# Half of the score masks by ScalarE and GpSimd, a first sequence without attention, start-up matmuls, and two PSUM banks each for attention and experts

## The reference

```
x = L0_attn_x                                   # (8, 256, 128)
# A: retention, 8 heads, key 16 wide, value 32 wide
qr, kr = rotate(q), rotate(k)                   # q*cos + swap_pairs(q)*sin
qk  = einsum('bhik,bhjk->bhij', qr, kr) * mask  # mask: causal decay
qk  = qk / clip(abs(qk.sum(-1)), 1.0)
out = einsum('bhij,bhjd->bihd', qk, v)
out = out * rsqrt(mean(out*out) + eps)
x   = x + (silu(g) * out) @ wo
# B: S = the 8 sequences, 16 heads, 4 key-value heads, head 8 wide
scores = where(causal, einsum(q, k) / sqrt(HD), min)
h1  = h + softmax(scores) @ v @ proj_weight.T
# C: router
logits = layer_norm(h1) @ router_weight ; top_p, top_i = top_k(softmax(logits), 2)
# M: experts, capacity 640 tokens
fc1 = gelu(xt @ moe_w1[e]) ; fc2 = fc1 @ moe_w2[e]
out = x + h1 + sum over the two experts of gate * fc2
```

## Time and profile before

| of the profiled execution | |
|---|---|
| its time | 242.57 us, of which the span of the trace is 240.8 us |
| TensorE clock granted, mean | 0.986 of full |
| PE busy | 216.7 us (90%) |
| PE weight loads busy | 183.6 us (76%) |
| DVE busy | 180.1 us (75%) |
| ACT busy | 146.1 us (61%), of which 46.2 us are 36 table loads |
| POOL busy | 94.8 us (39%) |
| first matmul starts at | 6.25 us |
| first expert matmul starts at | 48.0 us |

### The profile page before, as it was taken

One profiled execution on the slowest core, in us unless ns is written; L12 is line 12 of the kernel. 1 busy time (PEld: TensorE's weight loads), 2 busy tenths in 40 slices (PEclk: granted clock), 3 DMA queues, 4 the chain that ended last, 5 costly groups with the idle time before them and its releaser, 6 DMA issues.

```text
span 240.8 us, 4945 instructions
## 1 busy us (share of the span) xinstructions
PE 216.7 (90%) x1744; PEld 183.6 (76%) x1744; DVE 180.1 (75%) x543; ACT 146.1 (61%) x268; POOL 94.8 (39%) x121
## 2 busy tenths in 40 slices
PE   0677868899999999989999999999999989989995
PEld 0456545688887878877888889998798869879994
DVE  1466788695989789899996998697749864895533
ACT  2162763778868756946973876586746465827431
POOL 0021345334558642528623850582465136521000
PEclk9977999999999999999999999999999999999999
DMA  6992000000000000000000000000000000000000
GB/s 178 292 319 57 4 0 0 4 0 3 0 3 3 0 25 0 3 1 3 1 0 25 0 0 4 22 3 0 22 3 1 23 0 4 22 3 0 23 3 22
DMA packets 8073, 6.46 MB, mean 27 GB/s; under 512 B 752, under 2 KB 7152, under 8 KB 8048
## 3 DMA queue, kind: packets, MB, share of 16 engines
q1 hardware_dynamic: 8048, 6.14, 8.8%
HBM read 5.09 MB, written 1.05 MB: 25 GB/s over the span
## 4 chain that ended last, share of the span: by engine, by line
PE 54%; DVE 16%; issue 14%; POOL 9%; ACT 4%; DMA 1%; DVEq 0%; POOLq 0%; ACTq 0%
PE bank L773 16%; PE bank L784 13%; POOL prod L293 5%; PE bank L672 3%; DVE ao L930 3%; PE bank L621 3%; PE bank L699 3%; PE bank L638 2%; DVE res L1036 2%; PE bank L684 2%; ACT L445 2%; POOL qk L369 2%; PE bank L629 1%; PE bank L691 1%; DVE sm L866 1%
## 5 line engine op out<-in xcount | busy, mean ns | idle before, releaser
L773 PE MATMUL bank<-x2T,w 128*128 128x256 f32 x256 | 64.4, 386 | 1.6 <-DVE res L1036 1.6
L784 PE MATMUL bank<-w,hT 128*128 128x128 f32 x512 | 64.7, 277 | 0.0
L784 PEld LDWEIGHTS bank<-w,hT 128*128 128x128 f32 x512 | 61.7, 192 | 3.0 <-issue 1.1
L583 ACT ACTIVATE hT<-bank 128x512 f32<-128x512 f32 x64 | 37.5, 598 | 23.6 <-PE bank L773 23.5
L773 PEld LDWEIGHTS bank<-x2T,w 128*128 128x128 f32 x256 | 45.3, 190 | 8.1 <-DVE res L1036 3.1
L1036 DVE SCALAR_TENSOR_TENSOR res<-bank,gate,res 128x128 f32<-128x128 f32 x128 | 38.4, 341 | 16.7 <-PE bank L784 15.4
L445 ACT ACT_TABLE_LOAD x36 | 46.2, 1283 | 4.4 <-DVE mv L812 3.7
L293 POOL TENSOR_TENSOR prod<-qkv 128x128 f32<-128x128 f32 (+7 forms) x16 | 22.3, 1413 | 36.6 <-ACT qkv L455 36.6
L866 DVE TENSOR_TENSOR sm<-bank,con 128x512 f32<-128x512 f32 x32 | 19.9, 683 | 5.1 <-PE bank L672 5.0
L301 POOL TENSOR_TENSOR prodv<-attn_exp,qkv 128x128 f32<-128x128 f32 (+7 forms) x16 | 18.7, 1188 | 9.2 <-ACT attn_exp L551 9.2
L376 POOL TENSOR_TENSOR qkc<-qk,kcum 128x256 f32<-128x256 f32 x8 | 5.8, 730 | 31.0 <-DVE kcum L852 31.0
(11 more groups left out here) (109 smaller groups left out, 378.8 us busy)
## 6 DMA issues: line engine op xcount, KB each, us to landing
x<-in_x SPq DMA_DIRECT2D x8, 128.0 KB, 4.3
w<-in_w SPq DMA_DIRECT2D x1, 1024.0 KB, 5.8
...
```

The source lines that it names most:

```text
L583: eng.activation(hT[:, n % NM], m_banks[n % NM][:].rearrange("p (t n) -> p t n", t=NF), ACT.Gelu_apprx_tanh).then_inc(sem("gelu"), 1)
L773: last = mm(m_banks[n % NM][:, t * SLEN:(t + 1) * SLEN], w1[:, e, t * P:(t + 1) * P], x2T[:, i], start=True, stop=True)
L784: last = mm(m_banks[n % NM][:, c * D:(c + 1) * D], hT[:, n % NM, t, c * P:(c + 1) * P], w2[:, e, t], start=(t == 0), stop=(t == NF - 1))
```

## The change

- Masks: from the third sequence on (i >= 2) the four masks are split. Banks 2 and 3 are masked by DVE as before. Banks 0 and 1 are copied to SBUF by ACT (`a_lift`), and POOL multiplies the copies by the triangle in place (`a_cut`). The next sequence's `a_T` and `a_qk` wait for the copies. For the first two sequences DVE masks all four, in the order 2, 3, 0, 1.
- `a_out` is split: the state part and heads 4 to 7 run once the first two masks are there, heads 0 to 3 in `a_out_rest`.
- The first sequence's B has no scores, softmax or products: ACT copies its value row into the place of the attention result.
- `NB` is 2 and `NM` is 2.
- `a_rowsums` issues its two matmuls with 64 rows each, in separate halves of the array's rows and into separate banks (f0 and f1, now one tensor `front`).
- Six matmuls on a tile of zeros (`p_warm`): four ahead of the first `a_T`, two more before `a_kT:0` and `a_scores:0`. In `a_rstd` the table load stands ahead of the wait.
- `a_qkc`, `a_weight`, `b_core` of sequences 0 and 1 and the products of sequence 1 move from POOL to DVE.
- In B the scores are stored with the sequence index innermost, so `b_max` and `b_sum` read neighbours.
- `ORDER` is a new table.

```diff
-NB = 1
-NM = 3
+NB = 2
+NM = 2
+MASK_ORDER = (2, 3, 0, 1)
...
+p_warm:0 p_warm:1 p_warm:2 a_stats:0 p_warm:3 a_aggr:0 a_rstd:0 a_xh:0 a_T:0 a_xT:0 a_qk:0 a_vmm:0 a_rotate:0
+a_v:0 a_g:0 a_rotated:0 p_warm:4 a_tanh:0 a_kcum:0 a_kT:0 a_knat:0 a_qo:0 a_qkc:0 a_state_mm:0 a_silu:0
...
+            def a_cut(i):
+                if i < VECTOR_FIRST:
+                    return
+                for r in range(2):
+                    eng.wait_ge(sem("lifted"), lifts(i) + r + 1)
+                    heads_of = sm[:, r].rearrange("p c h n -> p (c h) n")
+                    eng.tensor_tensor(heads_of, heads_of, tri.unsqueeze(1).to_broadcast([P, 4, P]),
+                                      ALU.mult).then_inc(sem("cut"), 1)
...
+                exp_ln()
                 eng.wait_ge(sem("a_aggr"), NC * (group[-1] + 1))
                 if i == 0:
                     eng.wait_ge(sem("eps"), 2)
-                exp_ln()
...
+            def a_lift(i):
+                if i < VECTOR_FIRST:
+                    return
+                for r in range(2):
+                    eng.wait_ge(sem("scores"), 4 * i + r + 1)
+                    copy(sm[:, r].rearrange("p c h n -> p (c h n)"), score_banks[r][:], "lifted")
...
                 eng.wait_ge(sem("qkv"), i + 1)
+                if i == 0:
+                    for c in range(NC):
+                        own = b_banks[i][:, c * QKV + D + KVD:(c + 1) * QKV]
+                        copy(aon[:, c].rearrange("p (r f) -> p r f", r=QPK),
+                             own.unsqueeze(1).to_broadcast([P, QPK, KVD]), "own_value")
...
+            def p_warm(i):
+                if i == 0:
+                    eng.wait_ge(sem("warm"), 1)
+                mm(m_banks[0][:, 0:SLEN], warm[:, 0:P], warm[:], start=True, stop=True)
...
-                if i >= 1:
-                    eng.wait_ge(sem("sm"), 4 * (i - 1) + 1)
+                if 1 <= i <= VECTOR_FIRST:
+                    eng.wait_ge(sem("sm"), masks(i - 1) + 3)
+                if i > VECTOR_FIRST:
+                    eng.wait_ge(sem("lifted"), lifts(i - 1) + 1)
...
                 for u in range(2):
-                    last = mm(f1[:, u * SLEN:(u + 1) * SLEN], same_head[:, u * P:(u + 1) * P], qkc[:],
+                    rows = slice(u * D // 2, (u + 1) * D // 2)
+                    last = mm(front[:, u, 0:SLEN], same_head[rows, u * P:(u + 1) * P], qkc[rows, :],
                               start=True, stop=True)
...
             def a_out(i):
-                eng.wait_ge(sem("sm"), 4 * (i + 1))
+                eng.wait_ge(sem("sm"), masks(i) + 2)
+                eng.wait_ge(sem("state"), i + 1)
...
+                heads(i, range(4, RH))
+            def a_out_rest(i):
+                if i < VECTOR_FIRST:
+                    eng.wait_ge(sem("sm"), masks(i + 1))
+                else:
+                    eng.wait_ge(sem("cut"), lifts(i + 1))
+                heads(i, range(4)).then_inc(sem("o"), 1)
...
             def a_mask(i):
-                for r in range(4):
+                for r in MASK_ORDER if i < VECTOR_FIRST else (2, 3):
```

More of the change, by code:

```diff
@@ L53 @@
-a_weight:1 c_stats:0 c_aggr:0 c_rstd:0 a_g:2 a_qo:2 c_core:0 a_s2:2 a_og:1 c_T:0 c_x2T:0 a_wo:1 c_logits:0
-a_x1:1 m_fc1_0:0 a_aggr:6 c_best:0 a_tanh:2 c_where:0 c_ahead:0 b_stats:1 m_fc1_1:0 m_gelu_0:0 c_onehot:0
-b_aggr:1 c_half:0 a_aggr:7 m_fc2_0:0 b_sub:1 c_select:0 m_gelu_1:0 a_silu:2 c_base:0 c_rank:0 c_gsel:0
-a_scores:2 c_gate:0 m_acc_0:0 b_rstd:1 m_fc1_2:0 a_mask:2 b_core:1 a_T:3 b_T:1 a_xT:3 m_fc2_1:0 b_l1T:1 b_qkv:1
-m_acc_1:0 a_out:2 m_gelu_2:0 b_kv:1 m_fc2_2:0 b_prod:1 a_osq:2 b_scores:1 a_ms:2 b_hid:1 b_max:1 a_qk:3 a_tt:2
@@ L78 @@
-a_state_mm:6 b_aoT:3 a_kcum:6 a_qo:6 b_proj:3 a_state:6 a_wo:5 a_qkc:6 b_h1:3 c_base:2 c_stats:3 a_rowsums:6
-a_x1:5 b_rstd:4 c_base:3 c_aggr:3 m_fc2_6:1 a_silu:6 c_rstd:3 b_core:4 a_s2:6 m_acc_5:1 c_cum:2 a_scores:6
-c_core:3 m_acc_6:1 c_T:3 a_mask:6 m_fc1_0:2 m_gelu_7:1 c_x2T:3 a_T:7 m_gelu_0:2 c_logits:3 m_fc2_7:1 a_xT:7
-c_best:3 a_vmm:7 c_where:3 c_ahead:3 c_onehot:3 c_half:3 c_select:3 c_rank:3 c_gsel:3 m_fc1_1:2 b_stats:5
-c_gate:3 m_acc_7:1 b_T:4 m_fc2_0:2 b_aggr:5 b_l1T:4 a_v:7 b_qkv:4 m_acc_0:2 a_qk:7 b_kv:4 m_gelu_1:2 b_prod:4
@@ new lines @@
+a_mask:0 a_out:0 a_out_rest:0 a_T:1 a_xT:1 a_osq:0 a_qk:1 a_vmm:1 a_rotate:1 a_ms:0 a_v:1 a_tt:0 a_rotated:1
+a_ln:0 a_kT:1 a_kcum:1 a_rs:0 a_knat:1 a_weight:0 a_qo:1 a_state_mm:1 a_g:1 a_og:0 a_stats:4 a_qkc:1 a_wo:0
+a_tanh:1 a_silu:1 a_aggr:3 a_state:1 a_x1:0 a_rstd:2 a_rowsums:1 b_stats:0 a_s2:1 b_aggr:0 a_stats:5 b_sub:0
+b_rstd:0 a_stats:6 a_scores:1 a_aggr:4 b_core:0 b_hid:0 a_mask:1 b_T:0 a_xh:2 b_l1T:0 b_qkv:0 a_T:2 a_out:1
+a_xT:2 a_aggr:5 b_kv:0 a_out_rest:1 a_qk:2 a_osq:1 a_ms:1 a_rotate:2 b_aoT_mm:0 a_vmm:2 b_aoT:0 b_proj:0 a_tt:1
@@ new lines @@
+a_v:2 a_rotated:2 b_h1:0 a_g:2 a_ln:1 a_aggr:6 a_rs:1 a_kcum:2 a_kT:2 a_knat:2 a_weight:1 a_state_mm:2 c_stats:0
+a_qkc:2 a_og:1 a_xh:3 a_tanh:2 a_state:2 a_wo:1 a_qo:2 a_silu:2 c_base:0 a_rowsums:2 a_x1:1 a_stats:7 a_s2:2
+a_aggr:7 b_stats:1 a_scores:2 b_aggr:1 c_aggr:0 b_sub:1 a_lift:2 a_mask:2 a_cut:2 a_T:3 a_xT:3 a_qk:3 a_out:2
+a_xh:4 c_rstd:0 b_rstd:1 c_core:0 a_out_rest:2 a_rstd:4 b_core:1 a_vmm:3 a_osq:2 a_rotate:3 b_hid:1 c_T:0 a_ms:2
+a_v:3 c_x2T:0 b_T:1 a_rotated:3 c_logits:0 a_tt:2 b_l1T:1 m_fc1_0:0 c_best:0 a_ln:2 a_kcum:3 a_kT:3 a_rs:2
@@ new lines @@
+a_scores:4 m_gelu_7:0 a_lift:4 m_fc1_0:1 a_mask:4 a_cut:4 c_logits:1 b_max:2 m_fc2_7:0 a_T:5 b_exp:2 m_acc_7:0
+a_out:4 b_prodv:2 a_xT:5 c_best:1 b_rstd:3 c_where:1 a_out_rest:4 c_onehot:1 a_qk:5 c_select:1 c_ahead:1 c_cum:1
+b_ao:2 c_half:1 m_gelu_0:1 b_sub:3 a_vmm:5 c_base:1 c_rank:1 b_sum:2 a_v:5 m_fc1_1:1 b_core:3 c_gsel:1 b_hid:3
+m_fc2_0:1 m_gelu_1:1 c_gate:1 a_osq:4 a_g:5 m_acc_0:1 b_norm:2 a_ms:4 a_tanh:5 a_rotate:5 b_aoT_mm:2 m_fc1_2:1
+m_fc2_1:1 m_gelu_2:1 a_rotated:5 b_T:3 m_fc2_2:1 m_acc_1:1 b_l1T:3 a_xh:6 b_aoT:2 m_fc1_3:1 m_acc_2:1 a_tt:4
@@ new lines @@
+a_cut:5 a_T:6 m_acc_7:1 m_fc1_0:2 a_xT:6 a_mask:5 c_rank:2 a_qk:6 b_sub:4 b_max:3 b_rstd:4 a_out:5 c_gate:2
+a_rotate:6 b_exp:3 b_core:4 b_prodv:3 a_out_rest:5 b_T:4 m_gelu_0:2 m_fc1_1:2 b_ao:3 b_l1T:4 a_osq:5 a_vmm:6
+c_cum:2 a_rotated:6 b_qkv:4 a_v:6 b_sum:3 m_fc2_0:2 b_kv:4 b_norm:3 m_gelu_1:2 a_kcum:6 b_prod:4 a_kT:6
+b_aoT_mm:3 a_ms:5 a_knat:6 b_aoT:3 m_acc_0:2 b_proj:3 a_tt:5 m_fc2_1:2 b_h1:3 a_ln:5 a_g:6 c_stats:3 a_rs:5
+b_hid:4 c_aggr:3 m_acc_1:2 m_fc1_2:2 c_rstd:3 c_base:3 m_fc1_3:2 c_core:3 a_qkc:6 b_scores:4 c_T:3 m_gelu_2:2
@@ L205, in build @@
         eps = sb("eps", [P, 2])
+        warm = sb("warm", [P, SLEN])
         x = sb("x", [P, NSEQ, NC, D])
```

292 lines of the change are left out of this document (176 added, 116 removed).

## The result

The changed kernel takes 244.21 us (median of 4 runs, 244.12 to 246.56); the kernel before took 241.80 (4 runs, 240.42 to 244.35). The ratio is 1.0172, 95% interval 1.0107 to 1.0237: slower by 1.7%, where 239.7 was forecast. The ratios leave out executions that took over 1.5% longer than the fastest of the same kernel, so a ratio can differ from the quotient of two medians. The profiled execution has a span of 242.4 us against the 237.9 of the prediction's sum, so 4.5 us have to be found.

The account below looks back on a forecast made before the run. PE was taken to set the time from 48 us on, A's chain before. Start 53.0 + PE work 174.8 + bank waits 3.7 + other losses 3.5 + end 2.9 = 237.9, + 1.8 = 239.7 us; own range 237.7 to 244.

Parts of the forecast that it names:

- the prediction's sum: Whole kernel: 53.0 + 174.8 + 3.7 + 3.5 + 2.9 = 237.9 us of span, before 1.8 is added.
- the 1.27 of the row of like shape: POOL's cuts: 12 products of 1.27 us each, taken from the `wgt` row, 15 us in all.
- Rival 2: Experts: the two banks become the bound through late gelu or `m_acc`, over 247.4 us; chance 0.10.
- without the half clock: Start: scores:0 to scores:1 takes 11.6 us rather than 12.8, as zeros bring PE to full clock.
- what I took off for the start: Before the first scores: -1.28 us for the early table load, -2.6 for full clock, so scores:0 at 13.9.
- Rival 3: DVE and POOL: twelve more POOL operations each delay DVE about 0.6 us, 2 us reach PE, 241.7; chance 0.14.
- GpSimd's work at nothing on the path: POOL: gets 15 us of products and loses about 10, 100 us in all, costed at nothing on the path.
- The term 0.41 per sequence: `a_rowsums` on PE: half-high matmuls run beside each other, 0.45 us rather than 0.86, -3.3 in all.
- The term of 3.7 us: Two expert banks: each pure pair loses 0.29 us, 3.7 over the new order, all in sequences 3 to 7.
- the -2.4 us for B and C of the last sequences in two banks: From 173 to 216 us: two banks let B and C overlap, removing 2.4 us of PE's losses.

Follow-up runs that it names:

- tail_three_banks: Changed kernel with a third bank for the experts of the last sequence alone; 243.95 us, ratio 1.0130 to the kernel before.
- warm_many: Changed kernel with seventeen more zero matmuls in PE's pauses of the first 50 us; 243.23 us, ratio 1.0127 to the kernel before.
- cut_quarter: Changed kernel with POOL's mask products cut to 128 of 512 columns, the rest left unmasked; 245.40 us, ratio 1.0180 to the kernel before.
- three_and_acc: Changed kernel with POOL's delayed product, more zeros, third tail bank, and `m_acc_2:5` ahead of `b_scores:7` on DVE; 240.96 us, ratio 1.0036 to the kernel before.

## Why the prediction was wrong

**Right.** The path by which it reasoned stands. Scores:0 started at 14.1 us (13.9 predicted), scores:1 at 29.5 (29.7), the first `a_qk` took 1.13 us, the 42 table loads 1.283 each, `b_T` never waited for the gate, and the waits of PE's weight loads for `m_acc` in the tail are 0.22 to 0.23. The cuts take 1.09 us, less than the 1.27 of the row of like shape. Rival 2, the expert banks as the bound, did not come: a pair takes 3.68 us where 3.81 was worked out and 3.52 is PE's work, so a pair loses 0.16 and not 0.29. With clock and collision mended the kernel takes 240.1 us, and with the tail's third bank the 239.7 that were forecast. That it comes out so closely is in part luck: the terms for the row sums and for the two banks are wrong and cancel.

**The start, +1.6 us.** Scores:2 were to start at 44.8 and the first expert matmul at 53.0; they came at 46.5 and 54.6. The step that failed is "without the half clock": I took the zeros to settle the clock for good. They settle it until some 25 to 30 us; in the changed kernel's profile, after 2.6 us in which PE worked for 0.77, the clock was at 1.2 GHz for 6.8 us. The same start with the lower clock for 3.4 us (tail_three_banks) or not at all (warm_many) has the first expert matmul at 52.7 to 52.8, as predicted.

The base of the forecast had the same flaw. The trace of the kernel before that I read has the lower clock twice in its start, 6.8 us in all (granted clock 0.986, span 240.8); at a clock of 1.0 many executions of that kernel have a span of 238.0. So part of what I took off for the start the kernel before gets by itself in such executions.

**The collision, +2.4 us.** Rival 3 was the right mechanism. That its 2 us came close is luck, for the way they are made is wrong: it spread 0.6 us over each of twelve new POOL operations, and had a quarter of it reach PE. In fact a cut of the new operations to 0.41 us each gave nothing (cut_quarter), while an old one met two DVE operations, held them up by 2.6 us in a row, and PE, which waits for the first and for what stands behind both, lost 2.4 us at that one place. The forecast itself had put GpSimd's work at nothing on the path. Delays on the side cost nothing; what counts is whether a collision falls on the operation that PE needs next. I gave it 0.14 as a case of its own; beside the half clock it was part of the outcome.

The rule from the Trainium skill that the prediction cites (SBUF — State Buffer, Who interferes with whom) bears out: `aon` has two inputs in SBUF, the product reads SBUF. The trace agrees, 1.68 us against 0.43.

**Row sums, +1.4 us behind the first expert matmul.** The term 0.41 per sequence measured 0.13 in the trace (0.76 - 0.63), and next to nothing in time (187.9 against 187.8 us with whole rows). The nearest row, the scores with 16 and 32 rows, did not bear on a pair of 64 rows. Five sequences stand behind 54.6 us: 5 x (0.41 - 0.13) = 1.4. The other three belong to the start.

**Two banks, -1.7 us.** The term of 3.7 us scaled by 0.16/0.29 is 2.0 (an estimate; no run isolates it but for the tail, where a third bank gave 0.4 by the medians, 240.11 against 239.75, and 0.4 to 0.5 behind the first expert matmul).

**What is left.** 1.6 + 2.4 + 1.4 - 1.7 = 3.7 of the 4.5 us. Of the other 0.8, 0.2 are a slip of the prediction: 189.9 - 182.8 is 7.1 us lost behind the first expert matmul before, not 6.9. The remaining 0.6 are not placed. One term that failed there is the -2.4 us for B and C of the last sequences in two banks: from 173 to 216 us PE is idle for 2.1 us, and was for 2.4 before. It waits 0.66 us for an accumulation behind the reduction `b_scores:7`, then 0.34 for `c_T:6` and 0.42 for `c_logits:6`. How much of these 2.1 us is already in the term of the banks, the runs do not separate. The one try at the waits (three_and_acc) made them longer, so their cause stays open.

**Why the change brings nothing even when mended.** With clock, collision and tail mended it equals the kernel before, 1.0001. The new order with all masks on DVE takes 252.0 us, the new steps in the old order 252.1, both together some 8 less. So each part pays for what the other costs, with the order of the masks as a cost of its own in both trials. PE's total is what it was but for about 1 us of row sums (8 x 0.13); what the change gives is slack in A's chain, and PE sets the time from 48 us on in both kernels.
